# Sixteen-head attention over features: one norm chain for both streams, and the block bias laid down by TensorE

## What is computed

```python
def mp_normalize(x, axis):
    ...
    w = jnp.sqrt(jnp.sum(jnp.square(x.astype(jnp.float32)), axis=axis, keepdims=True))
    w = EPS + w / np.sqrt(red)
    return x / w.astype(x.dtype)
...
q = mp_normalize(q, axis=(3,))
k = mp_normalize(k, axis=(3,))
scores = jnp.einsum('bnsh,bnsk->bnhk', q, k / np.sqrt(S))
attn = jax.nn.softmax(scores, axis=3)
o = jnp.einsum('bnhk,bnsk->bnsh', attn, v)
```

## Time and profile before

| | us |
|---|---|
| median of 3 runs | 1864.93 |
| lowest and highest run | 1859.33, 1867.01 |
| the profiled execution, its own time | 1866.25 |
| its span in the profile | 1864.7 |

### The profile page before, as it was taken

How to read it: one execution, slowest core, us unless ns; L and a number is a source line. 1 busy time by engine, 2 the same in 40 slices (tenths; PEclk the granted TensorE clock), 3 DMA queues, 4 the chain that set the end, 5 groups by cost and what they waited for, 6 DMA issues and landing times. The chain is left out here.

```text
span 1864.7 us, 40486 instructions
## 1 busy us (share of the span) xinstructions
PE 1517.4 (81%) x17436; PEld 1275.1 (68%) x17436; DVE 1153.1 (62%) x2927; ACT 673.5 (36%) x1320; POOL 125.1 (7%) x265
## 2 busy tenths in 40 slices
PE   5787787787787657989876989986989985998986
PEld 3566566665565246969765978865978864887875
DVE  4755756756766876734575844576754556763665
ACT  2344344334344543522232532232532332342231
POOL 1011011011011000010000010010010010000000
PEclk9798798778898658999887998887998878898888
DMA  7000000000000001000000000000000000000000
GB/s 292 1 1 2 1 1 2 1 1 2 1 1 1 1 1 59 1 1 4 1 1 2 1 1 3 1 1 2 1 1 3 2 1 2 1 1 1 3 1 23
DMA packets 6369, 20.00 MB, mean 11 GB/s; under 512 B 2224, under 2 KB 4272, under 8 KB 5808
## 3 DMA queue, kind: packets, MB, share of 16 engines
q1 hardware_dynamic: 6192, 17.32, 2.5%
HBM read 16.27 MB, written 1.05 MB: 9 GB/s over the span
## 5 line engine op out<-in xcount | busy, mean ns | idle before, releaser
L464 PE MATMUL PS<-CC 128*128 128x256 f32 x616 | 192.1, 450 | 23.7 <-DVE xn L447 13.1
L464 PEld LDWEIGHTS PS<-CC 128*128 128x128 f32 x616 | 131.0, 230 | 43.1 <-issue 24.3
L562 PEld LDWEIGHTS PS<-vo,AR 128*64 128x64 f32 x2560 | 109.1, 170 | 29.8 <-ACT AR L523 15.1
L454 POOL TENSOR_SCALAR SC<-mv 128x2 f32<-128x2 f32 x96 | 18.7, 195 | 1641.3 <-DVE mv L443 1637.3
L562 PE MATMUL PS<-vo,AR 128*64 128x18 f32 x2560 | 121.7, 236 | 3.6 <-ACT AR L523 3.4
L1674 PE MATMUL PS<-AR,PA 64*64 64x204 f32 (+39 forms) x2624 | 120.5, 314 | 4.5 <-issue 4.5
L1658 PE MATMUL PS<-AR 64*64 64x32 f32 (+1 forms) x3072 | 116.9, 227 | 3.2 <-DVE AR L2020 2.3
L1658 PEld LDWEIGHTS PS<-AR 64*64 64x64 f32 x3072 | 113.2, 145 | 5.0 <-DVE AR L2020 3.2
L544 PE MATMUL PS<-CC,AR 128*128 128x128 f32 x512 | 100.2, 330 | 17.1 <-ACT AR L529 13.8
L474 PE MATMUL PS<-CC,xn 128*128 128x128 f32 x192 | 43.8, 313 | 83.2 <-DVE xn L447 82.2
L1674 PEld LDWEIGHTS PS<-AR,PA 64*64 64x64 f32 x2624 | 98.1, 139 | 14.0 <-issue 12.3
(11 more groups left out here) (407 smaller groups left out, 3219.5 us busy)
## 6 DMA issues: line engine op xcount, KB each, us to landing
WC<-in_cw SPq DMA_DIRECT2D x1, 5438.5 KB, 23.6
PA<-in_fd SPq DMA_DIRECT2D x1, 2624.0 KB, 9.3
AR<-in_stat SPq DMA_DIRECT2D x1, 2560.0 KB, 12.6
out<-X SPq DMA_DIRECT2D x1, 1024.0 KB, 5.1
PA<-in_aw SPq DMA_DIRECT2D x1, 975.0 KB, 11.1
AR<-in_raw SPq DMA_DIRECT2D x1, 832.0 KB, 8.0
CC<-in_const SPq DMA_DIRECT2D x1, 808.5 KB, 7.9
AR<-in_intw SPq DMA_DIRECT2D x1, 576.0 KB, 9.0
```

The source lines that it names most:

```text
L464: T.matmul(st.ps[:, bank, 0:ST], lhsT=ident, rhs=CC[:, 0:ST], start=True, stop=True)
L562: m = T.matmul(out_[rows, q // 2, r, :, h, :], lhsT=AT[:, o:o + SEQ], rhs=vo[:, q, r, :, h, :], start=True, stop=True)
```

## The change

The second half of the norm chain (the reciprocal root, the product, the scale and the inverse) is no longer issued once for each stream on 64 columns, but once for both on 2x64 columns of SC, after both streams' sums are there; the two writes of normed q and k follow it directly. VectorE's addition of head_bias is gone: TensorE writes head_bias (identity times head_bias, two matmuls of 128x256 for a stream) into banks 2 and 3 and adds the scores to it, and VectorE reads the maximum and the difference from these banks. For this the scores move from banks 0 and 1 to 2 and 3. A bank can take the bias only when ScalarE has copied v out of it, so TensorE waits for that copy (the new name `values`). Both streams' `keep_clock` and bias matmuls now stand ahead of stream 0's scores; the number of `keep_clock` matmuls is the same. The later `keep_clock` goes to bank 0.

```diff
-            keep_clock(st, 3, 3, 3)
+            for u in streams if st.s == 0 else ():
+                T.wait_ge(*u.act.at(f"{k}.values"))
+                keep_clock(u, 3, 3, 3)
+                for a in range(2):
+                    T.matmul(u.ps[:, 2 + a, 0:2 * P], lhsT=ident, rhs=bc(cc("head_bias"), 1, 2), start=True, stop=False)
             T.wait_ge(*st.dve.at(f"{k}.qk"))
             for q in range(SQ):
                 rows = slice(SEQ * (q % 2), SEQ * (q % 2) + SEQ)
-                m = T.matmul(ps[:, q % 2, (q // 2) * P:(q // 2 + 1) * P], lhsT=qf[rows, q // 2, 0:P],
-                             rhs=qf[rows, q // 2, P:2 * P], start=True, stop=True)
+                m = T.matmul(ps[:, 2 + q % 2, (q // 2) * P:(q // 2 + 1) * P], lhsT=qf[rows, q // 2, 0:P],
+                             rhs=qf[rows, q // 2, P:2 * P], start=False, stop=(q // 2 == 1))
             m.then_inc(*st.pe.up(f"{k}.scores"))
             yield
-            keep_clock(st, 2, 3, 0)
+            keep_clock(st, 0, 3, 0)
...
-            V.tensor_reduce(ss, sq, AX, ALU.add).then_inc(*v.up())
-            vector_rsqrt(v, st.sc[:, 256:320], st.sc[:, 64:128], st.sc[:, 320:384])
...
+            V.tensor_reduce(ss, sq, AX, ALU.add).then_inc(*v.up(f"{k}.sums"))
+            if st.s:
+                b, both = pair.dve, SC[:, :, 64:128]
+                for u in streams:
+                    V.wait_ge(*u.dve.at(f"{k}.sums"))
+                vector_rsqrt(b, SC[:, :, 256:320], both, SC[:, :, 320:384])
+                V.wait_ge(*b.now())
+                V.tensor_tensor(both, both, SC[:, :, 256:320], ALU.mult).then_inc(*b.up())
...
+                V.reciprocal(both, both).then_inc(*b.up())
+                V.wait_ge(*b.now())
+                for u in streams:
+                    V.tensor_tensor(u.ar[:, 0:512].rearrange("p (j n d) -> p j n d", j=TS, d=HD),
...
+                                    ALU.mult).then_inc(*u.dve.up(f"{k}.qk"))
             yield
             V.wait_ge(*st.pe.at(f"{k}.scores"))
-            V.tensor_tensor(g4, ps[:, 0:2, 0:2 * P].rearrange("p a (b n) -> p a b n", b=2),
-                            bc(bc(cc("head_bias"), 1, 2), 1, 2), ALU.add).then_inc(*v.up())
-            V.wait_ge(*v.now())
-            V.tensor_reduce(mx, g4, AX, ALU.max).then_inc(*v.up())
-            V.wait_ge(*v.now())
-            V.tensor_tensor(g4, g4, bc(mx, 3, P), ALU.subtract).then_inc(*v.up(f"{k}.below"))
+            scores = ps[:, 2:4, 0:2 * P].rearrange("p a (b n) -> p a b n", b=2)
+            V.tensor_reduce(mx, scores, AX, ALU.max).then_inc(*v.up())
+            V.wait_ge(*v.now())
+            V.tensor_tensor(g4, scores, bc(mx, 3, P), ALU.subtract).then_inc(*v.up(f"{k}.below"))
```

More of the change, by code:

```diff
@@ L810, in scalar_l0_attention @@
             A.square(sq, pq).then_inc(*a.up(f"{k}.squares"))
-            A.copy(ar[:, 1024:1024 + ST], ps[:, 2, 0:ST]).then_inc(*a.up())
+            A.copy(ar[:, 1024:1024 + ST], ps[:, 2, 0:ST]).then_inc(*a.up(f"{k}.values"))
             yield
@@ L837, in vector_l0_attention @@
             k, ps, ar, v = "L0a", st.ps, st.ar, st.dve
-            qk = ar[:, 0:512].rearrange("p (j n d) -> p j n d", j=TS, d=HD)
             sq = ar[:, 512:1024].rearrange("p (j n d) -> p j n d", j=TS, d=HD)
-            pq = ps[:, 0:TS, 0:2 * P].rearrange("p j (n d) -> p j n d", d=HD)
             ss = st.sc[:, 64:128].rearrange("p (j n) -> p j n", j=TS)
@@ L846, in vector_l0_attention @@
             V.wait_ge(*st.act.at(f"{k}.squares"))
-            V.tensor_reduce(ss, sq, AX, ALU.add).then_inc(*v.up())
-            vector_rsqrt(v, st.sc[:, 256:320], st.sc[:, 64:128], st.sc[:, 320:384])
-            V.wait_ge(*v.now())
-            V.tensor_tensor(st.sc[:, 64:128], st.sc[:, 64:128], st.sc[:, 256:320], ALU.mult).then_inc(*v.up())
-            V.wait_ge(*v.now())
-            V.tensor_scalar(ss, ss, float(1 / np.sqrt(HD)), 1e-4, ALU.mult, ALU.add).then_inc(*v.up())
-            V.wait_ge(*v.now())
@@ L854, in vector_l0_attention @@
-            V.reciprocal(ss, ss).then_inc(*v.up())
-            V.wait_ge(*v.now())
-            V.tensor_tensor(qk, pq, bc(ss, 3, HD), ALU.mult).then_inc(*v.up(f"{k}.qk"))
+            V.tensor_reduce(ss, sq, AX, ALU.add).then_inc(*v.up(f"{k}.sums"))
[7 more added lines that the diff above has]
+                V.wait_ge(*b.now())
+                V.tensor_scalar(both, both, float(1 / np.sqrt(HD)), 1e-4, ALU.mult, ALU.add).then_inc(*b.up())
+                V.wait_ge(*b.now())
+                V.reciprocal(both, both).then_inc(*b.up())
+                V.wait_ge(*b.now())
+                for u in streams:
+                    V.tensor_tensor(u.ar[:, 0:512].rearrange("p (j n d) -> p j n d", j=TS, d=HD),
+                                    u.ps[:, 0:TS, 0:2 * P].rearrange("p j (n d) -> p j n d", d=HD),
+                                    bc(u.sc[:, 64:128].rearrange("p (j n) -> p j n", j=TS), 3, HD),
+                                    ALU.mult).then_inc(*u.dve.up(f"{k}.qk"))
```

## The result

| | kernel before | changed kernel |
|---|---|---|
| median of 4 runs each, us | 1865.97 | 1889.19 |
| lowest and highest run | 1859.33, 1871.01 | 1883.71, 1893.68 |
| the profiled execution, its own time | 1866.25 | 1885.91 |
| ratio, with its 95% interval | | 1.0125 [1.0080, 1.0171] |

A forecast was written before the change was run, and what follows sets the result against it. No engine was full; VectorE bound loop A's stage, 14.48 us a trip. Chain 2.71 plus bias 1.43, less waits 0.59 and 0.81 or 0.30, gave about 11.5 us in four trips: 1853.5 us, eight-in-ten range 1847 to 1862.

The forecast's parts named there:

- The stage: Loop A, first L849 to first L875: 11.7 or 11.2 us where 14.48 stood, each trip gaining 2.74 or 3.25 us.
- The chain: Loop A's fourteen short VectorE instructions, joint for both streams: 5.03 us, 2.71 us less than two chains of 3.87.
- The reciprocal of 128 columns: In loop A's joint chain: 0.40 us for 64 columns more, at the rows' slope of 6.25 ns a column.
- The two new waits: VectorE in loop A waits 0.59 us for ScalarE's second square and 0.81 or 0.30 us for stream 0's scores.
- The maximum from PSUM: VectorE's maximum in loop A, read from PSUM, taken as dear as the one from the scratch area.
- The twenty passes: TensorE's bias and keep_clock passes ahead of stream 0's scores in loop A: about 4.9 us, hidden under the joint chain.
- the joint chain costs nearly two: Rival, chance 0.06: loop A's joint chain takes 7.74 us, a trip gains 0.03 us, and the time is 1864.8 us.
- more than planned: Rival, chance 0.12: TensorE keeps its clock up through loop A's scores and mixes; four trips give 16.2 us, 1848.7 us.
- The first rival: Chance 0.22: the mechanism holds, but under half a per cent is left after a loss over both loops; 1856 to 1862 us.
- nothing outside it changes by design: Outside loop A's stage of about 58 us of 1865, the edit was taken to change nothing.
- Sum: Loop A's gain of about 2.87 us a trip, 11.5 us in four, carried into the total: 1853.5 us, 0.61% faster.
- slower, by the clock: Rival, chance 0.08: loop A's new rhythm leaves TensorE at its lower clock more often; near 50 us over both loops, 1903.

The follow-up runs named there:

- the versions without the wait: Changed kernel with 4 or 14 memsets on VectorE ahead of loop C, two of the six with fewer keep_clock matmuls: mean 1864.8 us in 70 runs.
- the versions of the whole change with the wait: Changed kernel as it is, measured twice, and with 14 memsets behind loop C: 1.0125, 1.0076 and 1.0102 against the kernel before.
- the bias alone: Kernel before with only TensorE's bias, a chain for each stream, and two memsets ahead of loop C: 1877.52 us (1.0054), again 1885.02 us (1.0114).

## Why the prediction was wrong

**What held.** The stage: 11.27 to 11.80 us against the 11.2 or 11.7 that were worked out. The chain: 5.04 against 5.03. The reciprocal of 128 columns took 953 ns, 400 more than on 64, the 6.25 ns a column of the earlier trace rows; the Trainium skill, VectorE: DVE Perf Modes, section "First, the fixed hardware budget", would have made it more by its repeat count of 8, and the rows' slope was right. The other short instructions took 293 ns (68 more than on 64 columns) and 227 (32 more, 28 assumed). The two new waits: 0.61 to 0.70 us, and 0.22 or 0.73 where 0.30 or 0.81 stood; three trips in four were fast, not one. The maximum from PSUM cost what was assumed, 686 ns. The twenty passes were hidden. About 12.6 us were gained ahead of loop C, in a sum that said 11.5 (the chance of the clock is in it). The rivals "the joint chain costs nearly two" and "more than planned" were not what happened. The first rival, the mechanism holds but under half a per cent is left, is nearest to what the versions without the wait show (1864.8 us in the mean, where it said 1856 to 1862), though not for the changed kernel itself.

**The step that failed** is the last of the first part: "nothing outside it changes by design". The data and the order of loop C were unchanged, but its code had moved. The edit was counted by what its instructions do, in microseconds, and not by how many there are: sixteen operations less in a trip of loop A are a shift for all that stands behind. From this come 5.8 us of direct waits in loop C (nearly all in three of its four trips), and more by the clock. Over all runs, the versions of the whole change with the wait lie 1.5 below to 0.4 us above the line, those without it 2.5 to 6.5 below: some 5 us apart from the clock. Their half-clock time is 541 to 577 us against 518 to 534; the means are 552 and 527, and 25 us at half clock are 10 us by the line. Both together are the 14.6 us between the means, 0.8%. That the wait comes with a lower clock is shown in the changed kernel by the versions that differ in the place of the code alone (14 memsets ahead of the loop or behind it: 518 and 534 against 556; 25 us in the means, with a standard error near 6). In the kernel before, 114 memsets added only 10 us at half clock (528 against 518), less than two standard errors; with the four matmuls beside them it was 550. By what way the wait lowers the clock is only argued: TensorE stands 2 us longer at the trip's start, and a clock of 0.50 was granted after 3.42 us of idle time in the earlier trace rows.

The forecast was 1853.5 us. Of the 26 us from there to the mean of 1879.4, this step accounts for 14.6. The other 11 are the step "Sum", which carried the stage's gain of 11.5 us whole into the total: without the wait the mean is 1864.8 us, only 1.8 below the 1866.6 of the kernel before. Why stays open.

**The rival "slower, by the clock"** had 0.08 and a wrong place. It laid the lower clock to the rhythm of the stage in loop A, but the three trips of loop A that can be measured became shorter, and the loss came with the place of the code in loop C. In the profiled execution the loss was in loop C: 1152.34 us at 0.88 and 1187.52 at 0.86 are about 277 and 333 us at half clock (twice the time, times one less the clock). The 56 us more are 22 us by the line, a little more with the clock's unrounded values; with 5.8 for the wait this covers most of the 35.2.

**What stays open.** With the code in its place, the whole change should have given 0.994, and six measurements gave 0.9935, 1.0005, 1.0015, 0.9992, 1.0000 and 1.0011. Off the line they gain 2.5 to 6.5 us, of 12 in the stages, and their half-clock time is 0 to 16 us up. In the six profiles the stretch from loop A's first copy to loop C's takes 644 to 660 us, 651.5 in the mean. In the six profiles of the kernel before and its variants it takes 654 to 667, 661.7 in the mean, so the gain is made there. Loop C takes 1163 to 1177 us, where the kernel before and three variants of it with no such wait have 1152 to 1171. These ranges overlap, and one profile scatters by more than the 7 us in question. One thing can be read from the granted clock, taken in windows of 1 us. The four stages together hold 11 to 16 us of half-clock time in the six versions, and 20 to 27 in the kernel before and its variants with the same `keep_clock`. So some 10 of the 12 us that went were at the lower clock, and by the line such a cut would show as 8 us below it. Yet the half-clock time of the whole run did not fall by 10; it is 527 us in the mean of the six against 518. The two variants of the kernel before with more `keep_clock` show the same: 13 to 14 us in the stages, and 519 and 520 in all. What the stage gave back to the clock, the rest of the program took again, and why is not shown. What takes the rest of the gain was not found: not the wait for code, not TensorE's code (1.0013) and not its added work (1.0000, 1.0011). The same holds for the bias alone, whose 5.8 us turned into a loss at its first two measurements. No version that was tried is faster than the kernel before with certainty.

## What to carry to other kernels

Count an edit's instructions as well as their time. In a program whose loops fetch their code anew in each trip, every instruction removed or added moves that engine's code of every later loop, and a border between two pieces can fall right behind the place that the loop's jump goes to, where nothing covers the fetch. It shows as idle time that ends with "issue" at the same instruction in each trip, and as more packets in a queue of instructions; a few idle instructions ahead of the loop tell the place from the edit. And in a kernel whose time goes with the granted clock as this one's does, plot time against clock over all runs before a gain of half a per cent is believed or blamed.

## What the runs showed of the hardware

- VectorE waited 1.8 to 2.1 us for its code at a bad place, once a trip, in three of four trips (five profiles of kernels with the wait); in the first trip, which is entered without a jump, 0.2 us. Moving its code by 4 or by 14 instructions removed the wait; moving it by 114 in the kernel before made it.
- A packet of VectorE's code moved about 0.4 us after the first copy of a trip began, and the second copy, which had to wait, began 1.7 to 1.8 us after the packet (three profiles: changed kernel, 14 memsets behind the loop, 114 memsets in the kernel before).
- The instructions come in packets of 8 KB on one queue (30 for 0.25 MB) and of 16 KB on another (150 for 2.46 MB). Moving VectorE's code changed the number on the first alone.
- The time of the same program moves far with the clock. Runs of the kernel before range from 1845.97 to 1895.84 us, with mean granted clocks of 0.842 to 0.875. The time falls by 16 us for each 0.01 of clock, and what is left beside the line is a few microseconds.
- Two measurements of one kernel, of ten to twelve runs each on two chips, differed by 0.6 to 0.7% twice (0.9935 and 1.0005; 1.0054 and 1.0114). That is as much as their intervals allow, and more than the effect that was looked for.
